# Router logits by column tiles with early weights, and the first spread of dt moved to the last expert's loads

## The chip, the cores and the metric

One core of one Trainium2 chip runs the whole network in one launch. The metric is device time in microseconds (us), the median of three executions. The engines are TensorE (PE), VectorE (DVE), ScalarE (ACT), GpSimd (POOL) and SyncE (SP, which here only issues transfers). Each works through its own list in order and waits on semaphores for the others.

## The reference, cut to what matters

Two blocks on x of shape [4, 512, 128] (2048 tokens, D = 128) come one after the other. Block 0 is attention with a gated mixture of experts; block 1 is a four-layer selective scan (state space) as `s`, and a routed mixture as `g`:

```
xn = layernorm(x)                                # end of stage 3
s  = four scan layers(xn)                        # first pieces in stage 4, the rest stage 5
h  = xn * rsqrt(mean(xn*xn) + eps)               # router input
probs  = softmax(h @ router_w.T)                 # 8 experts
p, i   = top_k(probs, 2);  rw = p / sum(p)
routed = each expert takes its first 320 tokens; silu(xg@rg) * (xg@ru) @ rd, times rw, added back
g  = silu(silu(xn@sg) * (xn@su) @ sd + routed)   # a shared expert of 1024 hidden, 8 of 512
x  = x + s * g
```

Here 2048 tokens are 16 column groups of 128 (`NT` = 16), in four chunks of 512 (`XT[:, c, :]`, x with features on partitions). `CAP` is 320.

## The kernel before

The work is a chain of stages, each a block of five instruction lists, with a barrier between blocks. The change touches the end of stage 3 (attention output, gate and layer norm of x, until about 373 us) and stage 4 (373 to 561 us). Stage 5 is the scan.

**Stage 3.** VectorE takes mean and variance of x by chunk (`mw`, `rstw`), GpSimd turns them into factors (`factors`, L1206 to L1210: a pow, then a product), ScalarE applies them (`norm_x`, L1229), TensorE transposes (`turn_x`, L1300), and ScalarE copies to `XT` (`keep_x`, L1244).

**Stage 4.** SP first loads the router's weights `w_r`, the triangle `below`, and the shared expert's `w_sg`, `w_su`, `w_sd` (L1502, L1504). TensorE waits for the first two and makes the logits as sixteen small matmuls, one for each group of 128 tokens, with x as the stationary operand and 8 columns (L1662). VectorE squares xn and sums it (L1959, L1961), GpSimd takes the root (L1608, L1609), VectorE scales the logits (L1966) and works through softmax, the two choices and the ranks. Into this chain VectorE fits `hidden` (L1957), the product of the shared expert, which TensorE needs before it can go on: a pair of gate and up matmuls (`shared`, L1670, L1671) uses two banks in turn.

Between these pairs TensorE does the first pieces of the scan (taps: `first_xi`, L1691, whose weights GpSimd builds in L1616 from a broadcast row that SP loads). GpSimd then scatters each token's row to its two experts (L1627, 32 indirect transfers, held back in groups of 11 by `s_od`).

**The experts.** Eight experts run in four rounds of two (`i` = 0, 1), each with its own buffers. TensorE does the four gate and up pairs (L1769, L1770), fetches the next expert's rows by a transpose (L1761), does the next expert's first pair, and then this expert's down product (L1794). Before an expert's first pair it waits for all three weights on one semaphore:

```
pe.wait_ge(s_w8[i], q * 48 + 48)
```

SP's list in these rounds is, for each expert, the rows, then gate and up weights, then the down weight (`turn`, L1571). Ahead of them stand the first store and spread of B and C (L1554, L1559), the rows of experts 0 and 1, and the first store of dt with its spread into `dtr_even` (L1567, L1570): four loads of 512 KB. ScalarE reads `dtr_even` as its first step of stage 5, and stage 4 ends only when the spread is in.

Of the kernel before, what the change touches and what calls it, by code (L numbers as in the profile page):

```python
# [46 lines left out]
def build_stages(nc, A, out):  # L47
    keep = ExitStack()
    with keep:
# [18 lines left out]
        tap_dram = nc.dram_tensor("taps_of_layers", [3, P, 4, 256], fp32).ap()  # L68
        keepx = ExitStack()
        X = sb(keepx, "X", [P, NT, D])  # L70
        XR = sb(keepx, "XR", [P, NT, D + 2])
# [3 lines left out]
        with keep0:  # L75
# [1086 lines left out]

            st3 = ExitStack()
            with st3:
# [15 lines left out]
                neghalf = sb(st3, "neghalf3", [P, 4])  # L1180
# [11 lines left out]
                with nc.Block() as block:  # L1192
                    @block.sync
                    def _(sp):
                        sp.wait_ge(s_es[1], 16 * (BLOCKS // 2))
                        for b in range(B):
                            sp.dma_start(part(Y1, b), yt_dram[512 * b:512 * b + 512, :].rearrange("(k p) d -> p k d", p=P)).then_inc(s_acc[b], 16)

                    @block.gpsimd
                    def _(pool):  # L1200
                        link = Chain(pool, s_pch)
                        nc.gpsimd.indirect_dma_start(yt_dram[:, :], bass.IndirectOffsetOnAxis(ap=at_t[(BLOCKS - 1) % 3][:, 0:1], axis=0), eo[(BLOCKS - 1) % 2][:, :], None,
                                                     bounds_check=T - 1, oob_is_err=False).then_inc(s_es[(BLOCKS - 1) % 2], 16)
                        link(nc.gpsimd.memset(neghalf[:, :], -0.5))

                        def factors(b, moments, r, o, turn):  # L1206
                            c = slice(4 * b, 4 * b + 4)
                            pool.wait_ge(s_st, 4 * turn + b + 1)
                            link(nc.gpsimd.tensor_tensor(r[:, c], r[:, c], neghalf[:, :], ALU.pow))
# [10 lines left out]
                        for b in range(B):  # L1220
                            factors(b, mw, rstw, ofw, 1)

# [182 lines left out]
        dtr_even = top("dtr_even", [P, 8, 512])  # L1405
# [28 lines left out]
        with st4:  # L1434
# [10 lines left out]
            w_r = sb(st4, "w_r", [P, NE])  # L1445
            w_sg = sb(st4, "w_sg", [P, 1024])
            w_su = sb(st4, "w_su", [P, 1024])
            w_sd = sb(st4, "w_sd", [P, 8, D])
# [3 lines left out]
            below = sb(st4, "below_sb", [P, P])  # L1452
# [9 lines left out]
            neghalf = sb(st4, "neghalf4", [P, NT])  # L1462
# [11 lines left out]
            sq = hid[:, 1, 0:4, :].rearrange("p a (t d) -> p (a t) d", d=D)  # L1474
# [11 lines left out]
            s_wr = sem("router_loaded")  # L1486
            s_w4, s_w8 = sem("shared_loaded"), [sem(f"expert_loaded{i}") for i in range(2)]
            s_xg = [sem(f"rows_loaded{i}") for i in range(2)]
            s_lg4, s_sq4, s_ms4, s_rn4, s_x4, s_e4, s_sel, s_rk, s_rows = map(sem, ("logits4", "squares4", "meansq4", "rnorm4", "logits_shifted", "exps4", "selected", "ranks", "rows_known"))
# [8 lines left out]
            with nc.Block() as block:  # L1498
                @block.sync
                def _(sp):  # L1500
                    for dst, src in ((w_r[:, :], A["w_router"]), (below[:, :], A["below"])):
                        sp.dma_start(dst, src).then_inc(s_wr, 16)  # L1502
                    for dst, src in ((w_sg[:, :], A["w_sg"]), (w_su[:, :], A["w_su"]), (w_sd[:, :, :], A["w_sd"])):
                        sp.dma_start(dst, src).then_inc(s_w4, 16)  # L1504

# [46 lines left out]

                    sp.wait_ge(s_dbc, 1)
# [7 lines left out]
                    sp.wait_ge(s_scat, 16 * 2 * NT)  # L1561
                    sp.wait_ge(s_clr, 12)
                    for i in range(2):
                        load_rows(i, i)

                    sp.wait_ge(s_dt, 2)
                    sp.dma_start(dt_dram[0].rearrange("(h p) t -> p h t", p=P), dt[:, :, :]).then_inc(s_dst0, 16)  # L1567
                    sp.wait_ge(s_dst0, 16)
                    for j in range(4):
                        sp.dma_start(dtr_even[32 * j:32 * j + 32, :, :], dt_dram[0].rearrange("(g c) t -> c g t", c=32)).then_inc(s_dtr0, 16)  # L1570
                    def turn(q, more):  # L1571
                        for i in range(2):

                            if more:
# [6 lines left out]
                                load_gate_up(q * 2 + (2 + i), i)  # L1581
# [1112 lines left out]
```

## Time and profile before

| | us |
|---|---|
| median of 3 runs | 1299.53 |
| lowest and highest | 1299.25, 1301.14 |
| the profiled execution | 1300.58 |
| its span, first to last instruction | 1298.7 |
| stages 1 to 3 end | about 373 |
| stage 4 | 373 to 561 |
| stage 5 and the end | 561 to 1298.7 |

The profiled execution is a fourth one, with 1.9 us around its span. Busy shares are means over stages with different limits, so a change inside stage 4 is read from the stretches of stage 4. All times below are counted from the start of the span.

### The profile page before, as it was taken

To read this page: it belongs to the slowest core of one execution; us is meant where nothing else is said; L and a number is where in the kernel's file an instruction comes from. 1 tells how busy PE (TensorE), PEld (TensorE's weight loads), DVE (VectorE), ACT (ScalarE), POOL (GpSimd) and SP (SyncE) were. 2 spreads that over 40 slices of the span, in tenths; PEclk is the share of its full clock that TensorE was granted. 3 is DMA by queue.
4 is the path that set the end of the run, shared out by engine and by line. 5 is a ranking of instruction groups with operands and counts; after the bars stand their busy time and mean duration, and the time that the engine had idled before them with its cause. 6 is when DMAs were issued, how large, how long until landed. Compare 5 with 4: busy or idle time off the path is not lost. (4 is left out here: it accounts for less than half of the span.)

```text
span 1298.7 us, 21475 instructions
## 1 busy us (share of the span) xinstructions
PE 1148.5 (88%) x6651; PEld 610.9 (47%) x6651; DVE 1085.2 (84%) x1509; ACT 1042.7 (80%) x1803; POOL 945.7 (73%) x822
## 2 busy tenths in 40 slices
PE   6467999999669999977999999999999999999885
PEld 4462245455345556743445444444444454444442
DVE  8967989999664222359999999999999999999996
ACT  4336999999642243488999999999999999999992
POOL 6733444444442541477999999999999999999995
PEclk9786999999859999989999999999999999999998
DMA  2022234343146027334325423451444254234420
GB/s 66 28 95 94 81 89 126 115 127 98 37 159 218 21 66 178 111 89 98 91 60 108 113 64 68 106 126 53 87 110 93 59 109 112 67 64 106 108 66 16
DMA packets 87972, 119.51 MB, mean 92 GB/s; under 512 B 18171, under 2 KB 48359, under 8 KB 87488
## 3 DMA queue, kind: packets, MB, share of 16 engines
q1 hardware_dynamic: 81344, 100.90, 30.7%
q0 software_dynamic: 6528, 17.40, 4.5%
q8 instruction: 48, 0.79, 0.3%
q14 instruction: 52, 0.43, 0.1%
HBM read 92.09 MB, written 27.47 MB: 92 GB/s over the span
## 5 line engine op out<-in xcount | busy, mean ns | idle before, releaser
L2212 POOL TENSOR_TENSOR hcm<-hs,Cc 128x1024 f32<-128x1024 f32 x255 | 601.0, 2381 | 27.9 <-DVE hs L2595 19.7
L2595 DVE TENSOR_TENSOR_SCAN hs<-decay,dbx 128x512 f32<-128x512 f32 x512 | 587.1, 1200 | 26.2 <-ACT decay L2488 9.5
L2329 PEld LDWEIGHTS dbx<-ident_sb,scaled 128*128 128x128 f32 x2048 | 226.8, 142 | 288.9 <-DVE hs L2595 163.5
L2329 PE MATMUL dbx<-ident_sb,scaled 128*128 128x128 f32 x2048 | 311.7, 282 | 41.9 <-DVE hs L2595 38.6
L2470 ACT ACTIVATE scaled<-duT,BT 128x256 f32<-128x256 f32 x579 | 266.5, 505 | 0.2 <-PE dbx L2329 0.2
L2488 ACT ACTIVATE decay<-dtr_odd,a_all 128x512 f32<-128x512 f32 x256 | 178.3, 723 | 3.5 <-DMA dtr_odd<-dt_turn 2.4
L2488 ACT ACTIVATE decay<-dtr_even,a_all 128x512 f32<-128x512 f32 x256 | 177.8, 717 | 3.0 <-DVE hs L2595 1.7
L2347 PE MATMUL y_bank<-hcm,fold_sb 128*32 128x512 f32 x1024 | 138.7, 614 | 1.6 <-POOL hcm L2212 1.6
L1005 ACT ACTIVATE ex<-tt 128x2048 f32<-128x2048 f32 x64 | 123.2, 1925 | 2.5 <-DVE tt L1056 1.8
L2260 PE MATMUL slots<-XT,w_tap 128*128 128x512 f32 (+1 forms) x224 | 115.4, 597 | 3.1 <-DVE scaled L2586 2.9
L2197 POOL TENSOR_SCALAR scaled<-duT,BT 128x256 f32<-128x256 f32 x204 | 96.3, 487 | 0.0
L1055 DVE TENSOR_TENSOR tt<-bank_l,gt 128x512 f32<-128x512 f32 x128 | 87.0, 680 | 6.2 <-ACT gt L998 4.5
L998 ACT ACTIVATE gt<-bank_d,dgh 128x512 f32<-128x512 f32 x128 | 82.3, 708 | 7.7 <-PE bank_d L873 7.7
L1056 DVE SCALAR_TENSOR_TENSOR tt<-bank_l,gt 128x512 f32<-128x512 f32 x128 | 86.9, 679 | 0.0
L1957 DVE TENSOR_TENSOR hid<-sil,u_bank 128x512 f32<-128x512 f32 x32 | 22.0, 687 | 59.4 <-ACT sil L1814 37.7
L927 PE MATMUL bank_pv<-ex,v_head 128*32 128x512 f32 x512 | 68.8, 611 | 2.3 <-DVE ybig L1063 1.5
L2586 DVE TENSOR_TENSOR scaled<-slots,BT 128x1024 f32<-128x1024 f32 (+1 forms) x60 | 67.8, 1130 | 0.0
L1814 ACT ACTIVATE sil<-g_bank 128x512 f32<-128x512 f32 x32 | 19.1, 597 | 47.3 <-PE u_bank L1671 47.2
L2047 DVE TENSOR_TENSOR hid<-sil,u_bank 128x320 f32<-128x320 f32 x32 | 15.6, 487 | 48.8 <-ACT sil L1900 48.8
L1635 POOL DMA_INDIRECT shares_of_tokens<-eo,to_u x18 | 17.2, 956 | 51.8 <-ACT eo L1937 48.2
L1627 POOL DMA_INDIRECT expert_rows<-XR,rows_u x32 | 31.3, 978 | 31.1 <-PE o_bank L1678 21.8
L2347 PEld LDWEIGHTS y_bank<-hcm,fold_sb 128*32 128x32 f32 x1024 | 20.3, 108 | 48.4 <-issue 40.3
(386 smaller groups left out, 1886.3 us busy)
## 6 DMA issues: line engine op xcount, KB each, us to landing
Cc<-bc_turn SPq DMA_DIRECT2D x256, 64.0 KB, 2.2
dtr_even<-dt_turn SPq DMA_DIRECT2D x32, 512.0 KB, 8.6
dtr_odd<-dt_turn SPq DMA_DIRECT2D x32, 512.0 KB, 8.9
dt_turn<-dt SPq DMA_DIRECT2D x16, 512.0 KB, 2.8
hid<-in_conv_row SPq DMA_DIRECT2D x4, 512.0 KB, 5.3
shares_of_tokens<-zeros SPq DMA_DIRECT2D x2, 1024.0 KB, 8.0
w_rg<-in_w_rg SPq DMA_DIRECT2D x8, 256.0 KB, 2.9
w_ru<-in_w_ru SPq DMA_DIRECT2D x8, 256.0 KB, 3.1
```

The source lines that it names most:

```text
L998: nc.scalar.activation(gt[:, st % RING, :], bank_d[st % 2][:, :], ACT.Tanh, scale=dgh[:, i:i + 1]).then_inc(s_G, 1)
L1005: nc.scalar.activation(ex[:, (st // 4) % 2, j:j + 2, :, :], tt[:, i:i + 2, :, :], ACT.Exp).then_inc(s_E, 2)
L1055: nc.vector.tensor_tensor(tt[:, st % RING, 0, :], bank_l[st % 2][:, 0, :], gt[:, st % RING, :], ALU.add)
L1056: nc.vector.scalar_tensor_tensor(tt[:, st % RING, 1, :], bank_l[st % 2][:, 1, :], -1.0, gt[:, st % RING, :], ALU.mult, ALU.subtract).then_ ...
L2197: nc.gpsimd.tensor_scalar(scaled[buffer_of(l, n, k)][:, kk, :, j, :], duT[:, n % 2, kk, :].rearrange("p (g c) -> p g c", c=32), BT[:, n % ...
L2212: nc.gpsimd.tensor_tensor(hcm[:, r - 1:r + 1, :], hs[:, p % HR - 1:p % HR + 1, :], Cc[:, k:k + 1, :].broadcast_to([P, 2, 512]), ALU.mult). ...
L2260: last = mm(dst[h][:, d:512], w_tap[:, 3 - d, P * h:P * h + P], XT[:, n % 4, 0:512 - d], start=(d == 0), stop=(d == 3))
L2329: last = nc.tensor.transpose(dbx[bank_of[p]][:, P * kk:P * kk + P], scaled[buffer_of(l, b, k)][:, kk, g, :, :].rearrange("p j c -> p (j c) ...
L2347: last = mm(y_bank[h][32 * q:32 * q + 32, :], fold[:, :], hcm[:, ring_of(l, b, p + q), :], start=False, stop=(k == 3), tile_position=(0, 3 ...
L2470: nc.scalar.activation(scaled[buffer_of(l, n, k)][:, kk, :, j, :], duT[:, n % 2, kk, :].rearrange("p (g c) -> p g c", c=32), ACT.Copy, sca ...
L2488: nc.scalar.activation(dec[:, p % DR, :], dtr[b % 2][:, g, :], ACT.Exp, scale=a_all[:, l, 4 * g + k:4 * g + k + 1]).then_inc(s_dec, 1)
L2595: nc.vector.tensor_tensor_scan(hs[:, p % HR, :], dec[:, p % DR, :], dbx[bank_of[p]][:, :], 0.0, ALU.mult, ALU.add).then_inc(s_sc, 1)
```

## The change

Four things are done together.

1. `dtr_even` is allocated before stage 3, and the router's, the triangle's and the shared expert's weights live in it until the shared expert is over. Their five loads are issued in stage 3.
2. The router logits come from four matmuls of 512 columns, each in its own 32 columns of the array, with the weights stationary. ScalarE copies them, four transposes turn them back, and VectorE reads them from there. The factor of the second norm, `rn_x`, is computed by GpSimd in stage 3 from the variance and factor it has; VectorE's square and sum go.
3. `hidden` stands earlier in the routing chain; scatters are held back in groups of 13 in place of 11; the rows of experts 0 and 1 are loaded ahead of the store and spread of B and C.
4. Since `dtr_even` is in use during the shared expert, the first store and spread of dt move into SP's last turn, between the gate and up weights and the down weight of expert 7. SP's loop over rounds is written out.

```diff
@@ stage 3
+            dtr_even = keepd.enter_context(nc.sbuf_tensor("dtr_even", [P, 8, 512], fp32, side="right"))
+            w_sg = dtr_even[:, 0:2, :].rearrange("p a b -> p (a b)")
...
+            w_r, below = dtr_even[:, 6, 0:32], dtr_even[:, 6, P:2 * P]
...
+                        sp.wait_ge(s_pch, 1)
+                        for dst, src in ((w_r[:, 0:NE], A["w_router"]), (below, A["below"])):
+                            sp.dma_start(dst, src).then_inc(s_wr, 16)
+                        for dst, src in ((w_sg, A["w_sg"]), (w_su, A["w_su"]), (w_sd, A["w_sd"])):
+                            sp.dma_start(dst, src).then_inc(s_w4, 16)
...
+                        link(nc.gpsimd.memset(w_r, 0.0))
...
+                        def root_of_x(b, n):
+                            c = slice(4 * b, 4 * (b + n))
+                            link(nc.gpsimd.tensor_tensor(rn_x[:, c], rstw[:, c], rstw[:, c], ALU.mult))
+                            link(nc.gpsimd.tensor_tensor(rn_x[:, c], rn_x[:, c], mw[:, c, 1], ALU.mult))
+                            link(nc.gpsimd.tensor_scalar(rn_x[:, c], rn_x[:, c], 1.1920929e-07, None, ALU.add))
+                            link(nc.gpsimd.tensor_tensor(rn_x[:, c], rn_x[:, c], neghalf[:, 0:4 * n], ALU.pow))
...
                         for b in range(B):
                             factors(b, mw, rstw, ofw, 1)
+                            if b == 1:
+                                root_of_x(0, 1)
+                        root_of_x(1, 3)
@@ stage 4, SP
-                    for dst, src in ((w_r[:, :], A["w_router"]), (below[:, :], A["below"])):
-                        sp.dma_start(dst, src).then_inc(s_wr, 16)
-                    for dst, src in ((w_sg[:, :], A["w_sg"]), (w_su[:, :], A["w_su"]), (w_sd[:, :, :], A["w_sd"])):
-                        sp.dma_start(dst, src).then_inc(s_w4, 16)
...
-                    sp.wait_ge(s_dt, 2)
-                    sp.dma_start(dt_dram[0].rearrange("(h p) t -> p h t", p=P), dt[:, :, :]).then_inc(s_dst0, 16)
-                    sp.wait_ge(s_dst0, 16)
-                    for j in range(4):
-                        sp.dma_start(dtr_even[32 * j:32 * j + 32, :, :], dt_dram[0].rearrange("(g c) t -> c g t", c=32)).then_inc(s_dtr0, 16)
+                    def spread_first_dt():
+                        sp.wait_ge(s_dt, 2)
+                        sp.dma_start(dt_dram[0].rearrange("(h p) t -> p h t", p=P), dt[:, :, :]).then_inc(s_dst0, 16)
+                        sp.wait_ge(s_dst0, 16)
+                        sp.wait_ge(s_od, at(3, 1, 1))
+                        for j in range(4):
+                            sp.dma_start(dtr_even[32 * j:32 * j + 32, :, :], dt_dram[0].rearrange("(g c) t -> c g t", c=32)).then_inc(s_dtr0, 16)
...
                                 load_gate_up(q * 2 + (2 + i), i)
+                                if q == 2 and i == 1:
+                                    spread_first_dt()
                                 sp.wait_ge(s_ed, at(q, 2, i + 1))
                                 sp.wait_ge(s_clr, 1)
                                 load_down(q * 2 + (2 + i), i)
@@ stage 4, GpSimd
-                            if (NT * i + t) % 11 == 0:
-                                pool.wait_ge(s_od, at((NT * i + t) // 11, 1, 1))
+                            if (NT * i + t) % 13 == 0:
+                                pool.wait_ge(s_od, at((NT * i + t) // 13, 1, 1))
@@ stage 4, TensorE
-                    for t in range(NT):
-                        last = mm(r_bank[:, NE * t:NE * t + NE], XT[:, t // 4, P * (t % 4):P * (t % 4) + P], w_r[:, :], start=True, stop=True)
+                    for c in range(4):
+                        last = mm(r_bank[32 * c:32 * c + 32, :], w_r, XT[:, c, :], start=True, stop=True, tile_position=(0, 32 * c), skip_group_check=True)
+                    last.then_inc(s_lg4, 1)
+                    pe.wait_ge(s_lgk, 1)
+                    for t in range(4):
+                        last = nc.tensor.transpose(x_bank[:, P * t:P * t + P], lgT[:, P * t:P * t + P], ident[:, :])
                     last.then_inc(s_lg4, 1)
@@ stage 4, ScalarE
+                    act.wait_ge(s_lg4, 1)
+                    nc.scalar.activation(lgT[:, :], r_bank[:, :], ACT.Copy).then_inc(s_lgk, 1)
@@ stage 4, VectorE
-                    TT(sq[:, :, :], XN[:, :, :], XN[:, :, :], ALU.mult).then_inc(s_sq4, 1)
...
-                    link(TT(pr[:, :, :], r_bank[:, 0:NT * NE].rearrange("p (t e) -> p t e", e=NE), wide(cols[:, 0, :]), ALU.mult))
+                    link(TT(by_chunk(pr[:, :, :]), x_bank[:, :].rearrange("p (t c e) -> p t c e", t=4, c=4)[:, :, :, 0:NE], by_chunk(wide(rn_x[:, :])), ALU.mult))
...
+                        hidden(0, i)
                         link(nc.vector.tensor_reduce(cols[:, 5, :], cand[:, :, :], AX.X, ALU.max))
                         link(TT(oh[i][:, :, :], cand[:, :, :], wide(cols[:, 5, :]), ALU.is_equal))
...
-                        hidden(0, i)
```

## Rows read from the trace of the kernel before

**Rows 1.** The page, part 1: busy us, share of the span, instructions.
```profile
PE 1148.5 (88%) x6651; PEld 610.9 (47%) x6651; DVE 1085.2 (84%) x1509; ACT 1042.7 (80%) x1803; POOL 945.7 (73%) x822
```
**Rows 2.** Windows: length, busy by engine, PEclk, DMA share, GB/s.
```profile
375.00:400.00 25.00, 24.64 (x68) 14.48 (x69) 17.27 (x41) 4.58 (x7) 11.02 (x24) 0.77 1.05 342
400.00:490.00 90.00, 88.59 (x404) 53.71 (x402) 26.42 (x49) 28.68 (x47) 37.53 (x42) 1.00 0.25 77
```
**Rows 3.** Timeline around the start of stage 4: start, length, engine, line, operation.
```profile
371.02 1.11 PE L1300 MATMUL s_bank<-ident_sb,XR 128*128 128x128 f32 x4 [1.07 <-ACT XR L1229]
...
375.31 6.99 PE L1662 MATMUL r_bank<-w_r,XT 128*128 128x8 f32 x32 [3.17 <-DMA below_sb<-in_below]
...
382.16 2.05 PE L1670 MATMUL g_bank<-XT,w_sg 128*128 128x512 f32 x2
382.42 0.29 DVE L1966 TENSOR_TENSOR pr<-r_bank,cols 128x128 f32<-128x128 f32 x1 [3.65 <-PE r_bank L1662]
...
387.24 0.69 DVE L1957 TENSOR_TENSOR hid<-sil,u_bank 128x512 f32<-128x512 f32 x1
```
**Rows 4.** Windows, the slice in which the clock rose.
```profile
386.00:388.00 2.00, 1.95 (x5) 0.45 (x4) 1.86 (x6) 0.59 (x2) 0.09 (x1) 0.90 0.94 388
```
**Rows 5.** Timeline: the last `keep_x`, and column-tile matmuls in stage 5.
```profile
372.17 0.60 ACT L1244 ACTIVATE XT<-s_bank 128x512 f32<-128x512 f32 x1 [0.72 <-PE s_bank L1300]
...
576.78 1.93 PE L2340 MATMUL y_bank<-xc,eo 128*32 128x512 f32 x8
```
**Rows 6.** Timeline: GpSimd's factors in stage 3, and the pow of 16 columns.
```profile
365.82 1.01 POOL L1209 TENSOR_TENSOR rstw<-rstw,neghalf 128x4 f32<-128x4 f32 x1 [1.56 <-DVE rstw L1334]
...
367.14 1.65 ACT L1229 ACTIVATE XR<-X,ofw,rstw 128x128 f32<-128x128 f32 x4 [0.72 <-POOL ofw L1210]
...
378.33 2.90 POOL L1609 TENSOR_TENSOR cols<-cols,neghalf 128x16 f32<-128x16 f32 x1
```
**Rows 7.** Timeline: GpSimd's first tap weights.
```profile
383.13 2.96 POOL L1616 TENSOR_TENSOR w_tap<-w_in,hid 128x256 f32<-128x256 f32 x4 [1.89 <-DMA hid<-in_conv_row]
```
**Rows 8.** Timeline of SP's list: when each transfer is issued.
```profile
488.99 1.82 SPq L1570 DMA_DIRECT2D dtr_even<-dt_turn  x4
494.67 1.62 SPq L1545 DMA_DIRECT2D xg<-expert_rows  x3
496.64 0.34 SPq L1535 DMA_DIRECT2D w_rg<-in_w_rg  x1
...
539.53 0.39 SPq L1536 DMA_DIRECT2D w_ru<-in_w_ru  x1
542.31 0.38 SPq L1540 DMA_DIRECT2D w_rd<-in_w_rd  x1
```
**Rows 9.** Transfers: us from issue to landing; the first is `dtr_even`'s, the last `w_rd`'s.
```profile
DMA to landing us min/median/max: 4.7/8.0/11.0
...
dt_turn<-dt SPq DMA_DIRECT2D x1, 512.0 KB, 2.8
...
xg<-expert_rows SPq DMA_DIRECT2D x1, 65.0 KB, 6.7
...
w_rg<-in_w_rg SPq DMA_DIRECT2D x1, 256.0 KB, 6.0
...
DMA to landing us min/median/max: 2.6/2.9/4.2
```
**Rows 10.** Timeline, TensorE: down products of experts 0 to 2; expert 7's first gate.
```profile
497.01 3.04 PE L1794 MATMUL e_bank<-w_rd,hid 128*128 128x128 f32 x24
...
506.34 2.96 PE L1794 MATMUL e_bank<-w_rd,hid 128*128 128x128 f32 x24
...
514.59 3.04 PE L1794 MATMUL e_bank<-w_rd,hid 128*128 128x128 f32 x24
...
547.25 0.78 PE L1769 MATMUL g_bank<-xgT,w_rg 128*128 128x320 f32 x2
```
**Rows 11.** Timeline, TensorE: 24 passes after a long idle time.
```profile
48.57 4.49 PE L558 MATMUL s_bank<-ident_sb,prod 128*128 128x128 f32 x24 [12.95 <-POOL prod L399]
```

More of the change, by code:

```diff
@@ L68, in build_stages @@
         tap_dram = nc.dram_tensor("taps_of_layers", [3, P, 4, 256], fp32).ap()
+        s_wr, s_w4 = (keep.enter_context(nc.semaphore(name)) for name in ("router_loaded", "shared_loaded"))
         keepx = ExitStack()
         X = sb(keepx, "X", [P, NT, D])
+        rn_x = sb(keepx, "rn_x", [P, NT])
         XR = sb(keepx, "XR", [P, NT, D + 2])
@@ L1159, in _ @@
                         settle(2, UNITS - 1)
+            keepd = ExitStack()
+            keep.push(keepd)
+            dtr_even = keepd.enter_context(nc.sbuf_tensor("dtr_even", [P, 8, 512], fp32, side="right"))
+            w_sg = dtr_even[:, 0:2, :].rearrange("p a b -> p (a b)")
+            w_su = dtr_even[:, 2:4, :].rearrange("p a b -> p (a b)")
+            w_sd = dtr_even[:, 4:6, :].rearrange("p a (f d) -> p (a f) d", d=D)
+            w_r, below = dtr_even[:, 6, 0:32], dtr_even[:, 6, P:2 * P]
             st3 = ExitStack()
@@ L1208, in factors @@
                             pool.wait_ge(s_st, 4 * turn + b + 1)
-                            link(nc.gpsimd.tensor_tensor(r[:, c], r[:, c], neghalf[:, :], ALU.pow))
+                            link(nc.gpsimd.tensor_tensor(r[:, c], r[:, c], neghalf[:, 0:4], ALU.pow))
                             nc.gpsimd.tensor_tensor(o[:, c], o[:, c], r[:, c], ALU.mult).then_inc(s_fac, 1)
@@ L1404, in build_stages @@
         dbc = top("dbc", [P, 512])
-        dtr_even = top("dtr_even", [P, 8, 512])
         scaled_0 = top("scaled_0", [P, 4, 8, 4, 32])
@@ L1485, in build_stages @@
             sem = lambda name: st4.enter_context(nc.semaphore(name))
-            s_wr = sem("router_loaded")
-            s_w4, s_w8 = sem("shared_loaded"), [sem(f"expert_loaded{i}") for i in range(2)]
+            s_w8 = [sem(f"expert_loaded{i}") for i in range(2)]
             s_xg = [sem(f"rows_loaded{i}") for i in range(2)]
-            s_lg4, s_sq4, s_ms4, s_rn4, s_x4, s_e4, s_sel, s_rk, s_rows = map(sem, ("logits4", "squares4", "meansq4", "rnorm4", "logits_shifted", "exps4", "selected", "ranks", "rows_known"))
+            s_lg4, s_lgk, s_x4, s_e4, s_sel, s_rk, s_rows = map(sem, ("logits4", "logits_copied4", "logits_shifted", "exps4", "selected", "ranks", "rows_known"))
             s_dch, s_pch, s_clr, s_zf, s_scat = map(sem, ("vector_steps4", "pool_steps4", "cleared4", "rows_cleared_x_stored", "scattered"))
@@ L1551, in _ @@
                     sp.dma_start(tap_dram[2], tap_out[:, :, :]).then_inc(s_tap, 16)
+                    sp.wait_ge(s_scat, 16 * 2 * NT)
+                    sp.wait_ge(s_clr, 12)
+                    for i in range(2):
+                        load_rows(i, i)
                     sp.wait_ge(s_dbc, 1)
@@ L1584, in turn @@
                                 load_down(q * 2 + (2 + i), i)
-                    with sp.Fori(0, 3) as q:
+                    for q in range(3):
                         turn(q, True)
@@ L1606, in _ @@
                         nc.gpsimd.memset(xg[i][:, :, :], 0.0).then_inc(s_clr, 1)
-                    pool.wait_ge(s_ms4, 1)
-                    link(nc.gpsimd.tensor_scalar(cols[:, 0, :], cols[:, 0, :], 1.0 / D, 1.1920929e-07, ALU.mult, ALU.add))
-                    nc.gpsimd.tensor_tensor(cols[:, 0, :], cols[:, 0, :], neghalf[:, :], ALU.pow).then_inc(s_rn4, 1)
                     for l in range(4):
@@ L1734, in _ @@
                     pe.wait_ge(s_sel, 1)
-                    mm(x_bank[:, 0:P], below[:, :], sel[:, :, :].rearrange("p t e -> p (t e)"), start=True, stop=False)
+                    mm(x_bank[:, 0:P], below, sel[:, :, :].rearrange("p t e -> p (t e)"), start=True, stop=False)
                     mm(x_bank[:, 0:P], ones[:, :], cum[0][:, 0:NT, :].rearrange("p t e -> p (t e)"), start=False, stop=True).then_inc(s_rk, 1)
```

21 lines of the change are left out of this document (4 added, 17 removed).

## The prediction

> **What bounds the kernel now.** I read the page first: one core, TensorE busy for 88% of the span [rows 1]. What comes after 561 us is the state-space scan, which the change leaves alone; it touches the end of stage 3 (to 373 us), stage 4 (373 to 561 us), so I asked for the busy time by stretch in stage 4. From 375 us on TensorE is busy nearly without a gap, first at a mean granted clock of 0.77 beside full DMA engines, later at 1.00 [rows 2]. Stage 4 ends in a barrier, and every engine starts stage 5 behind it. What TensorE gains or loses inside stage 4 therefore moves the end of the kernel one for one, and I price each edit by when TensorE starts its next matmul.
>
> Then the timeline of the boundary. The last turn of x runs at 371.02 us, the next matmul at 375.31: TensorE waits for `w_r` and `below`, loaded only when stage 4 begins. Thirty-two 8-column matmul passes take 6.99 us, and the first matmul of the shared expert stands at 382.16; VectorE takes the logits at 382.42 [rows 3]. From there TensorE works through without a stall worth counting until the experts. The clock is at its lower level (1.2 GHz) until about 386.4 us: the slice from 386 to 388 us has a mean of 0.90 [rows 4]. So it rose some 4.2 us after 382.16, when dense matmuls had replaced the narrow ones.
>
> **Part A, the router at the front.** After the change the weights are in SBUF before stage 4, so TensorE starts with the first other engines, at about 373.3 us.
> - Four column-tile matmuls of 512 columns, eight passes, stand side by side. The nearest row is the same form (128x32 weights, 512 columns, eight passes) near a low clock: 1.93 us. The copy of 128x512 on ScalarE is the 0.60 us of `keep_x` [rows 5]. Four transposes at the lower clock are 1.11 us [rows 3]. With two hand-overs of about 0.05 us (the ScalarE copy at 372.17 begins as the modelled matmul end of 371.02 + 1.11 passes) that is 1.93 + 0.60 + 1.11 + 0.1 = 3.7 us.
> - What it costs ahead of that: GpSimd computes `rn_x` in stage 3. One pow of 4 columns is 1.01 us (365.82 to 366.83); the product behind it is over when ScalarE goes on at 367.14, so a small product with its gaps is about 0.28, and the new group `root_of_x(0, 1)` is 3 x 0.28 + 1.09 = 1.9 us. It starts at 364.3 and ends at 366.2, where the factors of the third group started at 365.82 and ScalarE stood waiting for them. So the stage-3 chain slips 0.4 us (0 if the gaps are shorter, 0.6 if longer). The last group is 12 columns; a pow of 16 columns took 2.90 us, so about 2.3, and 369.3 + 0.9 + 2.3 = 372.5 us, behind the last `keep_x` (372.8) and so hidden [rows 6].
> - Sum: 373.3 + 0.4 + 3.7 = 377.4 us for the first shared matmul, against 382.16. **Gain 4.7 us.** Bounds: 5.2 with nothing lost in stage 3; 4.0 if the clock rises later after a front that is now broken up by a hand-over (1.4 us more at half clock would cost 0.7).
> - Does it stay? VectorE drops a product and a sum over 2048 elements that were hidden anyway, and its first `hidden`, which stood 4.8 us behind the start of the routing chain [rows 3], now stands three steps earlier in it. Even at the old distance it runs from 377.6 + 4.8 = 382.4 to 383.1, and TensorE needs it only after two pairs of gate and up, 5.8 us in the kernel before (382.16 until that `hidden` was over at 387.93): 383.2. The tap weights could become the next wait: GpSimd began them at 383.13 when the broadcast row landed, 2.96 us for four [rows 7]. That load is now issued about 1.9 us earlier with 1.5 MB less in front. Landing at 378.5 to 381.2 gives taps at 381.5 to 384.2, against a need at 377.4 + 5.8 + 1.7 = 384.9. Covered, narrowly at one end.
> - The five loads moved into stage 3 stand behind the four loads of Y1 in an idle queue; nobody there waits behind them. Scatters regrouped from 11 to 13 end sooner and the expert rows were not late before: worth nothing. Storing and spreading B and C behind the rows is hidden too, since Cc is read in stage 5 alone.
>
> **Part B, the early spread goes.** Before, SP issued the four 512 KB loads of `dtr_even` from 488.99 us; the rows of the third expert were issued at 494.67 [rows 8]. The last spread load landed 11.0 us after its issue at about 490.4, so at 501.4, and the rows landed 6.7 us after theirs, at 501.4 as well [rows 9]. The first expert's down product starts at 497.01, the second's 9.33 us later, the third's 8.25 us after that [rows 10]. The period without the collision is 8.25. **Gain 1.1 us** (0.9 to 1.3).
>
> **Part C, where the spread goes to.** This edit decides. `spread_first_dt` is now issued inside the last turn of SP's list, between `load_gate_up` and `load_down` of the last expert. Ahead of `load_down(7, 1)` stand a 512 KB store, a wait for its landing, and the four loads. TensorE needs all three weights of expert 7 before its first gate product: `s_w8[1]` must reach 192, which counts `w_rd`. That product ran at 547.25 us [rows 10], and `w_rd` had been issued at 542.31 [rows 8] and landed in 2.9 [rows 9], about 2 us ahead. On the time scale of before:
> - store issued at 540.0 us, behind `w_ru` (issued 539.53). It alone took 2.8 us [rows 9], giving 542.8; behind two 256 KB loads still moving until about 542.1, I take 544.0.
> - the first spread load goes at 544.0, and the last lands 501.4 - 488.99 = 12.4 us later, at 556.4. `w_rd`, issued at 546.1 (the four issues take 1.82 us [rows 8]), is behind it: `w_rg` of before, issued next after the rows, landed at 496.64 + 6.0 = 502.6, 1.2 us after them [rows 8, 9]. I take 1.0: 557.4.
> - TensorE stands still from 547.25 to 557.4. **Loss 10.1 us** (8.9 if the store lands at 542.8; 10.6 if the homeward scatters of GpSimd slow it). Nothing hides it: TensorE issues in order, the down product of expert 6 is behind the same wait, and ScalarE, VectorE and the barrier behind that.
>
> The Trainium skill (DMA: Bandwidth & Descriptors, "Queues, rings and completion order") says that descriptors are consumed in ring order on each engine, and SP owns one row of rings. By that rule `w_rd` cannot pass the spread; the trace agrees, with the rows and the last spread load both landing at 501.4 us. Without the rule the forecast would be the first rival below.
>
> - **The clock after that stall.** After 12.95 us of idling, TensorE's 24 passes at 48.57 us took 4.49 us [rows 11], where 24 passes take 3.0 in the experts [rows 10]: 1.5 us lost. The rise at 386.4 came after 4.2 us at half clock, 2.1 us lost. **Loss 1.8 us** (1.0 to 3.0).
>
> The Trainium skill (TensorE: Matmul & The Clock Gate, "What's actually happening") says that the slow clock is the default and activity releases it. By that rule an idle stretch is paid again when work comes back; the trace agrees with the 1.5 us above. A sum that left it out would be 1.8 us lower.
>
> **Sum.** -4.7 - 1.1 + 10.1 + 1.8 = +6.1 us. The profiled execution took 1300.58 us in all, 1.05 above the median of the three runs; applied to the median, 1299.53 + 6.1 = 1305.6 us. With all bounds on one side: +3.4 (1302.9) to +8.7 (1308.2); that is the likeliest case's own range.
>
> **Rivals.**
> - *`w_rd` overtakes the spread* (ends on the other side). If transfers of one queue share the engines instead of queueing, `w_rd` is issued at 546.1 and lands 4.2 us later, the longest of its six [rows 9]: 550.3, a stall of 3.1 with hardly a clock to lose: -4.7 - 1.1 + 3.1 = -2.7, 1296.8 us. It decides for faster once `w_rd` lands before about 553 us on the old scale. Against it: the rows and the spread's end coincide. For it: the two loads differ in shape. With it goes the case that I misplace the need and TensorE waits later. Chance 0.12.
> - *The front gives nothing.* If the column tiles ran one after another, eight passes at half clock (the 2.05 us pair [rows 3] times four, 8.2 us) take 6.3 us more than assumed, and A turns into a loss of 1.6: +12.4, 1311.9 us. Milder: the taps late by 1 to 2 us or the clock late, A of 2 to 3 us, about 1308. For it: the taps have 0.7 us of cover at one end. Against: the column-tile row. Chance 0.10.
> - *The stall is shorter than I sum*, by a faster late spread, since then the experts' loads are nearly over: 7 us and 1 of clock, +2.2, 1301.7 us. Against it: the early one moved alone for most of its time as well. Chance 0.10.
> - My forecast: 0.68.
>
> **Numbers.** A measurement of this kernel tells about 0.2%, 2.6 us, from no change: 1296.9 to 1302.1. The overtaking case lies half below that; the short stall is inside. Faster 0.09, same 0.15, slower 0.76. The range takes in the forecast's bounds, most of the short stall and the milder front loss: 1301.0 to 1309.0, leaving out the overtaking case and the serial tiles.
>
> **What would show it.** Right: the first shared matmul 4 to 5 us earlier; no wait for rows at the third expert; SP's list with store, spread, then `w_rd` last; a TensorE wait of 9 to 10 us on `w_rd` ahead of the eighth expert's gate product; a clock of 0.5 behind it. Wrong: `w_rd` landing ahead of the last spread load; a wait for the broadcast row at the taps; transposes of the logits that start after 377 us.

## The result, and the profile after

| | before | after |
|---|---|---|
| median of 10 runs each, us | 1300.38 | 1304.21 |
| lowest and highest, us | 1299.25, 1302.78 | 1303.93, 1305.44 |
| profiled execution, its span, us | 1300.58, 1298.7 | 1305.44, 1303.6 |

The ratio of the times is 1.0031, with a 95% interval of 1.0022 to 1.0040: slower by 0.3%, on the forecast's side of the 0.2% bound. The sum had said 1305.6 us, and the range 1301.0 to 1309.0.

The front in the profile after, from the timeline (start, length, engine, line, operation, idle time and its releaser):

```profile
371.64 0.60 ACT L1270 ACTIVATE XT<-s_bank 128x512 f32<-128x512 f32 x1 [0.73 <-PE s_bank L1326]
...
373.28 1.94 PE L1676 MATMUL r_bank<-XT,dtr_even 128*32 128x512 f32 x8 [1.68 <-PEq L1202]
...
375.92 1.11 PE L1680 MATMUL x_bank<-ident_sb,logits_by_expert 128*128 128x128 f32 x4 [0.71 <-ACT logits_by_expert L1826]
...
376.83 1.92 PE L1688 MATMUL g_bank<-XT,dtr_even 128*128 128x512 f32 x2
...
377.42 0.73 POOL L1630 TENSOR_TENSOR w_tap<-w_in,hid 128x256 f32<-128x256 f32 x1 [1.00 <-DMA hid<-in_conv_row]
```

The four column tiles take 1.94 us, and the first shared matmul stands at 376.83, where it stood at 382.16 [rows 3]: 5.3 us earlier. Of these, 0.8 were there before the change begins (the same instruction of stage 3, ahead of GpSimd's new steps, stood at 360.13 before and at 359.36 after), so the front itself gave 4.6. Below, profiles are laid against each other at ScalarE's last copy of stage 3, the first line here (371.64; 372.17 before, [rows 5]). The tap weights begin at 377.4, 5.7 us ahead of [rows 7]. Neither they nor the first `hidden` (381.18) hold TensorE up.

The clock, from the windows of the profile after (length, busy by engine, PEclk, DMA share, GB/s):

```profile
380.00:382.00 2.00, 2.00 (x4) 0.87 (x3) 1.51 (x5) 0.60 (x1) 0.29 (x1) 0.63 1.01 427
382.00:384.00 2.00, 2.00 (x6) 0.89 (x5) 1.79 (x7) 0.60 (x1) 0.00 (x0) 1.00 0.38 61
...
544.00:546.00 2.00, 0.00 (x0) 0.00 (x0) 0.00 (x0) 0.00 (x0) 0.00 (x0) 0.83 1.10 206
546.00:548.00 2.00, 0.00 (x0) 0.00 (x0) 0.00 (x0) 0.00 (x0) 0.00 (x0) 0.50 1.04 239
...
554.00:556.00 2.00, 2.00 (x12) 1.88 (x12) 0.00 (x0) 0.11 (x1) 0.00 (x0) 0.61 0.00 0
556.00:558.00 2.00, 2.00 (x12) 1.59 (x13) 0.00 (x0) 0.87 (x3) 0.00 (x0) 1.00 0.00 0
```

The clock rose in the slice from 380 us, some 4.6 us after the first shared matmul (4.2 before). It fell to its lower level in the slice from 544 us, when TensorE had idled since 540.6, and was back at 2.4 GHz by 556.

The experts, TensorE's timeline after:

```profile
491.51 3.04 PE L1812 MATMUL e_bank<-w_rd,hid 128*128 128x128 f32 x24
...
508.00 3.04 PE L1812 MATMUL e_bank<-w_rd,hid 128*128 128x128 f32 x24
...
539.86 0.70 PE L1788 MATMUL u_bank<-xgT,w_ru 128*128 128x320 f32 x2
550.37 1.41 PE L1787 MATMUL g_bank<-xgT,w_rg 128*128 128x320 f32 x2 [9.81 <-DMA w_rd<-in_w_rd]
...
552.63 4.37 PE L1812 MATMUL e_bank<-w_rd,hid 128*128 128x128 f32 x24
556.93 0.81 PE L1787 MATMUL g_bank<-xgT,w_rg 128*128 128x320 f32 x2
...
561.72 3.07 PE L1812 MATMUL e_bank<-w_rd,hid 128*128 128x128 f32 x24 [1.05 <-DVE hid L2064]
566.93 1.50 PE L2346 MATMUL dbx<-ident_sb,scaled 128*128 128x128 f32 x12 [2.15 <-PEq L1516]
```

Each stage of the sum can be read off against [rows 10]. The first down product is 5.50 us earlier, the third 6.59: the early collision is gone, 1.1 us. Then comes the wait of 9.81 us, named as forecast, and expert 7's first gate product is 3.12 us later than before instead of 6.6 earlier, so the stall took 9.7. From it to the pair behind the down product are 6.56 us; before they were 4.04 (547.25 to 551.29), so the low clock took 2.5. Stage 5 begins 5.6 us later than at 561.30; in this execution it was itself 0.7 us shorter, so the span grew by 4.9.

SP's list after, and how long two of its transfers took:

```profile
532.90 0.43 SPq L1581 DMA_DIRECT2D dt_turn<-dt  x1
537.18 1.83 SPq L1585 DMA_DIRECT2D dtr_even<-dt_turn  x4
539.11 0.53 SPq L1553 DMA_DIRECT2D w_rd<-in_w_rd  x1
```

```profile
dt_turn<-dt SPq DMA_DIRECT2D x1, 512.0 KB, 4.3
...
w_rd<-in_w_rd SPq DMA_DIRECT2D x1, 256.0 KB, 11.2
```

`w_rd`, 256 KB, is issued at 539.11 and lands 11.2 us later, at 550.3, where it took 2.9 [rows 9]. The last of the spread's four loads lands at about 549.7 (issued at 538.6, 11.1 us to its landing), ahead of it.

### The profile page after: what moved, and what is told of

The parts are those of the page before. It is cut to its first block and busy times, and to the rows that moved or that the text cites. A ratio compares the mean times of both kernels' runs of the same rounds, so it can differ in the third digit from the quotient of the medians.

```text
span 1303.6 us, 21361 instructions
## 1 busy us (share of the span) xinstructions
PE 1148.3 (88%) x6631; PEld 609.1 (47%) x6631; DVE 1079.6 (83%) x1507; ACT 1042.5 (80%) x1804; POOL 945.8 (73%) x828
```

## The experiments

My theory: the front and the lost collision give some 6 us, and the stall of TensorE on `w_rd` with its clock takes some 12. Rivals: the end of stage 4 is set by something else, so that taking the stall away gives back less; and the front gives less or more than its parts.

**x1. The spread behind the down weight.**

```diff
                                 load_gate_up(q * 2 + (2 + i), i)
-                                if q == 2 and i == 1:
-                                    spread_first_dt()
...
                                 load_down(q * 2 + (2 + i), i)
+                                if q == 2 and i == 1:
+                                    spread_first_dt()
```

> The changed kernel with the store and spread of dt moved by one place, behind the load of expert 7's down weight. Queue theory (the loss is only w_rd's place behind the store and the spread): the wait of 9.8 us and the 2.5 us of low clock behind it go; GpSimd's scatters home still share the engines with the spread and may now end the stage, costing 0 to 1.5 us. 1304.2 - 12.2 + 0.8 = about 1293 us (1291.5 to 1295). Load theory (2 MB late in stage 4 hurt wherever they stand, by full transfer engines): most of the loss stays, 1300 us or more. Time theory (the spread would now be late for stage 5): a ScalarE wait ahead of the first decay, 1297 or more.

Measured: 1296.47 us, ratio 0.9971 (0.9961 to 0.9981). The wait on `w_rd` is gone, yet only two thirds of the 12 us came back: above the range of the Queue theory, and well below the 1300 us of the Load theory. The timeline of x1:

```profile
544.19 3.66 POOL L1661 TENSOR_SCALAR scaled<-duT,BT 128x256 f32<-128x256 f32 x8 [4.85 <-DMA shares_of_tokens<-eo,to_u]
...
547.92 3.07 PE L1812 MATMUL e_bank<-w_rd,hid 128*128 128x128 f32 x24 [1.05 <-DVE hid L2064]
...
550.65 0.93 POOL L1666 DMA_INDIRECT shares_of_tokens<-eo,to_u  x1 [0.30 <-issue]
...
556.27 3.41 PE L2346 MATMUL dbx<-ident_sb,scaled 128*128 128x128 f32 x16 [5.28 <-PEq L1516]
```

TensorE is done at 550.99 and waits 5.28 us at the barrier, where it waited 2.16 before. GpSimd is the late one. It waits for the scatters of expert 5's rows to land, 4.85 us (before: 1.62), where the spread is in flight beside them (x11 gives the 1.62 us back with no spread there); then it computes `scaled_0` for 3.66 us, and only then issues the scatters of expert 6. From the end of its last one (551.58) to stage 5 are 4.69 us. That distance is 4.68 us before the change (556.62 to 561.30) and in the profile after (562.25 to 566.93), too. The prediction left this list out.

**x2. The spread ahead of the rounds, as before the change.** 
```diff
-                                if q == 2 and i == 1:
-                                    spread_first_dt()
...
+                    spread_first_dt()
                     for q in range(3):
                         turn(q, True)
```

> The changed kernel with the store and spread of dt ahead of the expert rounds, as in the kernel before. Queue theory: no wait for w_rd, and the 1.1 us wait of the third expert's rows is back: 1304.2 - 12.2 + 1.1 = about 1293 us (1292 to 1296). The front's gain then stands alone against the kernel before: 5 to 7 us faster. If the front had gained nothing: 1300.

Measured: 1295.83 us, ratio 0.9960 (0.9946 to 0.9975). TensorE's timeline of x2:

```profile
490.38 3.04 PE L1811 MATMUL e_bank<-w_rd,hid 128*128 128x128 f32 x24
...
496.68 0.64 PE L1778 MATMUL x_bank<-ident_sb,xg 128*128 128x128 f32 x3 [1.99 <-DMA xg<-expert_rows]
...
500.82 1.39 PE L1811 MATMUL e_bank<-w_rd,hid 128*128 128x128 f32 x11
```

The first two down products are 10.44 us apart in place of 8.24: the early collision costs 2.2 us here, since TensorE arrives sooner; the expectation had 1.1 for it, and its range held. There is no stall at the end.

**x3. The late spread alone**, moved in the kernel before, whose front stays as it was.

```diff
@@ kernel before
+                    def spread_first_dt():
...
                                 load_gate_up(q * 2 + (2 + i), i)
+                                if q == 2 and i == 1:
+                                    spread_first_dt()
```

> The kernel before with one edit only: the store and spread of dt in the last turn, ahead of expert 7's down weight. Queue theory: +9.7 (wait) + 2.5 (clock) - 1.1 (early collision gone) = +11.1, about 1311.5 us (1309.5 to 1313). If the loss needed the other edits (the weights' new place, the reordered queue): less than +5.

Measured: 1311.60 us, ratio 1.0082 (1.0064 to 1.0100). TensorE's timeline of x3:

```profile
554.70 1.41 PE L1772 MATMUL g_bank<-xgT,w_rg 128*128 128x320 f32 x2 [10.15 <-DMA w_rd<-in_w_rd]
```

TensorE waits 10.15 us for `w_rd`. The harm needs none of the other edits: the spread's place alone costs 10.7 us net by the ratio (8.3 to 13.0).

**x4. The down weight on a semaphore of its own.** The gate product needs `w_rg` and `w_ru` alone; only the down product waits for `w_rd`. The transfers stand as after.

```diff
-                            pe.wait_ge(s_w8[i], q * 48 + 48)
+                            pe.wait_ge(s_w8[i], q * 32 + 32)
...
+                            pe.wait_ge(s_wd[i], q * 16 + 16)
                             pe.wait_ge(s_hd8, n(4, 4))
```

> The changed kernel with the down weight on a semaphore of its own, which TensorE waits for ahead of the down product instead of ahead of the first gate product. The transfers keep their order. Queue theory: w_rd lands at about 550.3 us, needed at about 549.4 now, so a wait of some 1 us, no low clock, GpSimd perhaps the last: 1293 to 1296 us. Load theory: full engines still delay what comes, 1300 or more.

Measured: 1298.32 us, ratio 0.9985 (0.9971 to 0.9998); the time lies over 2 us above the expected range. The timeline of x4:

```profile
547.83 3.68 POOL L1661 TENSOR_SCALAR scaled<-duT,BT 128x256 f32<-128x256 f32 x8 [7.42 <-DMA shares_of_tokens<-eo,to_u]
549.90 3.07 PE L1813 MATMUL e_bank<-w_rd,hid 128*128 128x128 f32 x24 [1.96 <-DMA w_rd<-in_w_rd]
...
554.30 0.94 POOL L1666 DMA_INDIRECT shares_of_tokens<-eo,to_u  x1 [0.30 <-issue]
...
559.93 2.37 PE L2347 MATMUL dbx<-ident_sb,scaled 128*128 128x128 f32 x10 [6.96 <-PEq L1516]
```

TensorE waits only 1.96 us for the weight and is done at 552.97. Then it waits 6.96 us for GpSimd, whose last scatter ends at 555.24, 4.69 us ahead of stage 5. So the stall on `w_rd` had hidden a second one, on the scatters home, and this bears out x1's reading.

**x5. x1, with `scaled_0` computed between the issue of expert 5's scatters and the wait for them.**

```diff
-                    def send_home(q, i):
+                    def send_home(q, i, meanwhile=lambda: None):
...
+                        meanwhile()
                         pool.wait_ge(s_eh, q * 96 + 48 * (i + 1))
...
+                    send_home(2, 1, first_scaled)
```

> The first experiment (spread behind the down weight) with one more edit: GpSimd computes its eight parts of scaled_0 while expert 5's scatters home are in flight, not behind their landing. In the first experiment GpSimd's last scatter stood 7.8 us behind the start of expert 6's down product, against 4.6 where no spread was in flight, and stage 5 started 4.65 us after GpSimd's last scatter in every trace. Theory (GpSimd's list, held up by scatters that share the engines with the spread, ended stage 4): 3.1 us less, about 1293.4 us (1292.5 to 1295). Rival (the spread's own landing or a second wait ends the stage): within 1 us of the first experiment's 1296.5.

Measured: 1293.71 us, ratio 0.9943 (0.9929 to 0.9956). The timeline of x5:

```profile
540.63 3.66 POOL L1660 TENSOR_SCALAR scaled<-duT,BT 128x256 f32<-128x256 f32 x8
...
547.75 1.06 POOL L1671 DMA_INDIRECT shares_of_tokens<-eo,to_u  x1 [3.46 <-DMA shares_of_tokens<-eo,to_u]
...
550.38 0.94 POOL L1671 DMA_INDIRECT shares_of_tokens<-eo,to_u  x1 [0.30 <-issue]
...
556.00 3.13 PE L2351 MATMUL dbx<-ident_sb,scaled 128*128 128x128 f32 x16 [3.76 <-PEq L1516]
```

The wait at the barrier shrank from 5.28 to 3.76 us by a change of GpSimd's order alone; its last scatter again ends 4.68 us ahead of stage 5. GpSimd's list sets the end of stage 4: in all thirteen profiles its last scatter ends 4.67 to 4.69 us ahead of stage 5, also in x1, x4 and x5, where TensorE's own wait is 5.28, 6.96 and 3.76 us instead of the 2.15 of the others. What fills these 4.68 us is not shown.

The profile has 1.5 us of gain over x1 where the expectation had 3.1: expert 5's scatters landed 7.16 us after the end of their issue here and 4.85 in x1, and why is not shown. The ratios differ by 3.6 us, with some 2 us of noise either way, which leaves room for both. So the direction is shown and the size is not.

**x6. TensorE kept busy through the wait**, by eleven matmuls of no use ahead of it. They write a bank that is written anew before it is read.

```diff
                             pe.wait_ge(s_tc, at(q, 2, i + 1))
+                            if i == 1 and isinstance(q, int) and q == 3:
+                                for _ in range(11):
+                                    mm(x_bank[:, :], ident[:, :], XT[:, 0, :], start=True, stop=True)
                             pe.wait_ge(s_w8[i], q * 48 + 48)
```

> The changed kernel with 11 extra matmuls of 512 columns (22 passes, about 9.5 us at full clock) into a free bank ahead of TensorE's wait for expert 7's weights; their result is read by nobody. Clock theory: the wait's end stays (w_rd's landing), the clock stays at full, and the 24 passes of the down product take 3.0 us, not 4.4: 2.5 us less, about 1301.7 us. Rival (what follows the wait is slow for another reason, such as full transfer engines): no change, 1304.2.

Measured: 1303.77 us, ratio 1.0022 (1.0013 to 1.0032). TensorE's timeline of x6:

```profile
539.27 9.60 PE L1787 MATMUL x_bank<-XT,ident_sb 128*128 128x512 f32 x22
549.34 0.81 PE L1790 MATMUL g_bank<-xgT,w_rg 128*128 128x320 f32 x2 [0.47 <-DMA w_rd<-in_w_rd]
...
550.52 2.97 PE L1815 MATMUL e_bank<-w_rd,hid 128*128 128x128 f32 x24
...
563.41 1.50 PE L2349 MATMUL dbx<-ident_sb,scaled 128*128 128x128 f32 x12 [2.15 <-PEq L1516]
```

The weight comes no sooner (58.96 us behind the first down product, 58.86 after), the granted clock is 1.00 in every slice from 538 to 552 us, and from the gate product to stage 5 are 14.07 us, where the profile after has 16.56 and the one before 14.05: in the profile, the 2.5 us are the clock's. The times say less. Their median is nearer the rival's 1304.2 than the 1301.7 expected, and the profiled execution is the fastest of the ten. By the ratios the gain is 1.2 us with some 1.7 of noise either way: it holds both nothing and 2.5.

**x7. The sixteen small matmuls of before**, all else as after; ScalarE's copy goes too, and VectorE reads `r_bank`.

```diff
-                    for c in range(4):
-                        last = mm(r_bank[32 * c:32 * c + 32, :], w_r, XT[:, c, :], start=True, stop=True, tile_position=(0, 32 * c), skip_group_check=True)
...
-                        last = nc.tensor.transpose(x_bank[:, P * t:P * t + P], lgT[:, P * t:P * t + P], ident[:, :])
+                    for t in range(NT):
+                        last = mm(r_bank[:, NE * t:NE * t + NE], XT[:, t // 4, P * (t % 4):P * (t % 4) + P], w_r[:, 0:NE], start=True, stop=True)
```

> The changed kernel with the logits as before, sixteen matmuls of 8 columns, from the weights loaded early, and no copy and no transposes. By the rows: 7.0 us in place of 3.6 from the first logits matmul to the first shared one, so +3.4: about 1307.5 us (1306 to 1309). Rival (the column tiles gain nothing, the early weights everything): 1304.

Measured: 1309.46 us, ratio 1.0066 (1.0050 to 1.0081). TensorE's timeline of x7:

```profile
372.53 6.97 PE L1676 MATMUL r_bank<-dtr_even,XT 128*128 128x8 f32 x32 [1.68 <-PEq L1202]
379.35 2.05 PE L1684 MATMUL g_bank<-XT,dtr_even 128*128 128x512 f32 x2
```

6.82 us from the first logit to the shared expert in place of 3.55: the new form gives 3.3 us here, and 4.0 until the first down product (122.18 us from the first logit, 118.23 after). By the ratios it gives 4.5, so the time lies a little above the expected range.

**x8. The five weight loads at the head of stage 4**, all else as after.

```diff
@@ stage 3, SP
-                        for dst, src in ((w_r[:, 0:NE], A["w_router"]), (below, A["below"])):
-                            sp.dma_start(dst, src).then_inc(s_wr, 16)
...
@@ stage 4, SP, its first instructions
+                    for dst, src in ((w_r[:, 0:NE], A["w_router"]), (below, A["below"])):
+                        sp.dma_start(dst, src).then_inc(s_wr, 16)
+                    for dst, src in ((w_sg, A["w_sg"]), (w_su, A["w_su"]), (w_sd, A["w_sd"])):
+                        sp.dma_start(dst, src).then_inc(s_w4, 16)
```

> The changed kernel with the five weight loads back at the head of stage 4; column tiles stay. By the rows: TensorE waits until 375.3 of before, 2.0 us later than now, and the broadcast row for the taps lands some 5 us later but still in time: +2.0, about 1306.2 us. If the taps become the wait: 1307 to 1309. Rival (the weights' load was hidden by something else): 1304.

Measured: 1307.48 us, ratio 1.0052 (1.0037 to 1.0067). TensorE's timeline of x8:

```profile
370.53 0.60 ACT L1265 ACTIVATE XT<-s_bank 128x512 f32<-128x512 f32 x1 [0.73 <-PE s_bank L1321]
...
373.70 1.93 PE L1676 MATMUL r_bank<-XT,dtr_even 128*32 128x512 f32 x8 [3.21 <-DMA dtr_even<-in_below]
...
378.94 2.07 PE L1688 MATMUL g_bank<-XT,dtr_even 128*128 128x512 f32 x2 [1.47 <-DMA dtr_even<-in_w_sd]
```

Two waits instead of one: 3.21 us for `below`, and 1.47 for `w_sd`, since logits that are done sooner meet shared weights that are not there. The expectation left out the second one.

From the last copy of stage 3 to the first shared matmul are 8.41 us here and 5.19 after, so the loads' place gives 3.2 us (2.7 by the ratios). The bare times, 378.94 and 376.83, differ by 2.1 only because stage 3 ended 1.1 us sooner in this execution. The same distance is 9.99 us before and 8.47 in x7. So neither edit has one price: the early loads give 1.5 us with the old logits and 3.2 with the new ones, and the new logits give 1.6 with late loads and 3.3 with early ones. Together they give 4.8.

**x9. Only the store of dt moved ahead of the rounds**; the spread stays where after has it.

```diff
                     def spread_first_dt():
-                        sp.wait_ge(s_dt, 2)
-                        sp.dma_start(dt_dram[0].rearrange("(h p) t -> p h t", p=P), dt[:, :, :]).then_inc(s_dst0, 16)
...
+                    sp.wait_ge(s_dt, 2)
+                    sp.dma_start(dt_dram[0].rearrange("(h p) t -> p h t", p=P), dt[:, :, :]).then_inc(s_dst0, 16)
                     for q in range(3):
```

> The changed kernel with only the store of dt moved ahead of the expert rounds (it finds an idle queue); the four spread loads keep their place ahead of w_rd. Queue theory: SP no longer stops for the store's landing, so the spread is issued at 532.9 us in place of 537.2, its last load and w_rd land 4.3 us earlier, and the wait is 5.5 us in place of 9.8: 4.3 us less, 1299.9 us (1299 to 1301); a shorter idle time may save some clock too. Load theory (the bytes late in stage 4 are the cost): 1303 or more, since only 0.5 MB moved away.

Measured: 1302.06 us, ratio 1.0015 (1.0004 to 1.0026). The timeline of x9:

```profile
532.31 1.94 SPq L1583 DMA_DIRECT2D dtr_even<-dt_turn  x4
535.06 0.40 SPq L1553 DMA_DIRECT2D w_rd<-in_w_rd  x1
...
546.94 1.41 PE L1787 MATMUL g_bank<-xgT,w_rg 128*128 128x320 f32 x2 [7.04 <-DMA w_rd<-in_w_rd]
```

The wait is 7.04 us in place of 9.81: not the whole of the store's 4.3 comes back, and the time lies 1 us above the expected range, yet below the Load theory's 1303 as well. Counted from the first down product the spread goes out 4.2 us sooner, but from its issue to the end of the wait are 14.6 us, where after has 13.2. Here the spread stands directly behind `w_rg` and `w_ru`, issued at 531.21 and 531.78, which may slow its start; no run tests that. `w_rd`, issued at 535.06, lands last again, 11.8 us later.

**x10. `hidden` back in its old place, and the scatters in groups of 11.**

```diff
-                            if (NT * i + t) % 13 == 0:
-                                pool.wait_ge(s_od, at((NT * i + t) // 13, 1, 1))
+                            if (NT * i + t) % 11 == 0:
+                                pool.wait_ge(s_od, at((NT * i + t) // 11, 1, 1))
...
-                        hidden(0, i)
                         link(nc.vector.tensor_reduce(cols[:, 5, :], cand[:, :, :], AX.X, ALU.max))
...
+                        hidden(0, i)
```

> The changed kernel with hidden back at the end of each choice and the scatters back in groups of 11. Both were priced at nothing: TensorE's third pair needs the first hidden 0.3 to 1.0 us after it is over, and the last scatter ends some 10 us ahead of the first expert's rows. 1304.2 us, within 0.7. Rival: with the front 5 us earlier the later hidden holds TensorE up, up to 1 us, and the scatters hold up the rows, 1 to 3 us more.

Measured: 1306.20 us, ratio 1.0044 (1.0030 to 1.0059). TensorE's timeline of x10, and below it the same pair in x11:

```profile
382.51 1.12 PE L1688 MATMUL g_bank<-XT,dtr_even 128*128 128x512 f32 x2 [0.84 <-DVE hid L1977]
```

```profile
381.71 1.12 PE L1688 MATMUL g_bank<-XT,dtr_even 128*128 128x512 f32 x2
```

The third shared pair waits 0.84 us for `hidden`. The profile after is no measure for that, since its clock rose 2.2 us later: its third pair starts at 382.58, no sooner than here. In x11 the clock rose as early as here and `hidden` stands in its new place, and from the first logit to the first down product are 117.44 us, here 118.21. So the place of `hidden` is worth 0.8 us where the clock rises early, and by these rows nothing where it rises as late as in the profile after: even in its old place the first `hidden` is over at 382.46, ahead of 382.58. The last scatter of rows went out at 471.98 us in place of 466.84, and no row was late for it.

The time lies 1.3 us above the expected range, on the side of the rival. By the ratios the two edits give 1.7 us, with some 2 of noise either way, so no more than the 0.8 can be assigned.

**x11. The spread taken apart**: dt stored ahead of the rounds, and one of the four loads behind the down weight of each of the first four turns.

```diff
                                 load_down(q * 2 + (2 + i), i)
+                                if q < 2:
+                                    spread_part_of_dt(2 * q + i)
```

> The kernel after with dt stored ahead of the rounds and its spread taken apart: one 512 KB load behind the down weight of each of the first four turns, none in the last. My account: what costs is the pile of four loads in front of a weight or a row that is needed soon. One load has to pass in the 3.1 us between the down weight and the next rows, and the rows have some 7 us until TensorE turns them. Then no wait on xg or w_rd appears on TensorE, the down products stand 8.24 us apart throughout, GpSimd's wait for the scatters of expert 5 is 1.6 us as before, and stage 5 begins 63.2 us after the first down product (65.4 in x2, less its collision of 2.2): span about 1290 to 1292, time about 1293.5 us, ratio 0.9945. Rival: any 2 MB of spread costs its share wherever it stands, since each later transfer of the turn is moved back: then the 2.2 us of x2 come back in small waits and the time is that of x2, about 1296 us (0.996).

Measured: 1293.70 us, ratio 0.9950 (0.9937 to 0.9964). The timeline of x11:

```profile
490.73 3.04 PE L1812 MATMUL e_bank<-w_rd,hid 128*128 128x128 f32 x24
...
493.80 0.38 SPq L1553 DMA_DIRECT2D w_rd<-in_w_rd  x1
494.27 0.45 SPq L1583 DMA_DIRECT2D dtr_even<-dt_turn  x1
496.69 1.33 SPq L1558 DMA_DIRECT2D xg<-expert_rows  x3
...
541.75 3.66 POOL L1661 TENSOR_SCALAR scaled<-duT,BT 128x256 f32<-128x256 f32 x8 [1.62 <-DMA shares_of_tokens<-eo,to_u]
...
553.92 1.50 PE L2346 MATMUL dbx<-ident_sb,scaled 128*128 128x128 f32 x12 [2.15 <-PEq L1516]
```

Stage 5 begins 63.19 us after the first down product (65.39 in x2, 75.42 after), GpSimd's wait is 1.62 us as before the change, and TensorE waits for no transfer. The same 2 MB cost nothing that is seen when they pass one part at a time. This version and x5 are faster than the kernel before by 0.50% and 0.57%, alike within their intervals.

## Why the prediction came right

- **The bound** (TensorE inside stage 4) held up to the last expert. What ends the stage it left out: GpSimd's last scatter, 4.67 to 4.69 us ahead of stage 5 in all thirteen profiles. In the change itself this costs nothing beyond the forecast, since those scatters wait for expert 6's down product and slip with it. It cost me the expectations of x1 and x4.
- **Part A**, 4.7 us: the profile has 4.6 at the first shared matmul. Its terms miss a little and cancel. The first logit comes 1.5 us sooner behind stage 3 where the sum had 2.0, the logits take 3.3 us less where it had 3.15, and stage 3 slips 0.2 where it had 0.4. "Eight passes side by side" held (1.94 us against 1.93 in [rows 5]). The Trainium skill (TensorEngine Tiling (Array Packing), "Key Properties") says that tiles operate independently and can work in parallel; the trace agrees, since one full matmul of two passes takes as long (1.92 us). What the sum did not have: the clock mostly rose sooner than assumed (below). With an early rise, as in x11, A is 5.5 us at the first down product instead of the 4.7 of the profile after, and the move of `hidden`, priced at nothing, is worth 0.8 of them.
- **Part B**, 1.1 us: measured 1.1. It was a lower figure than the collision is worth behind the new front (2.2, x2).
- **A and B together** are x11: 6.5 us by its ratio (4.7 to 8.2), 6.6 by its profile, where the sum had 5.8.
- **Part C, the stall**, 10.1 us: the profile has 9.7. The store took 4.3 us (assumed: 4.0), `w_rd` was issued 6.2 us behind it (6.1) and landed last, as the prediction had it: 11.2 us for 256 KB.
- **Part C, the clock**, 1.8 us: the profile has 2.5, above the middle of its bounds of 1.0 to 3.0.
- **C over many runs** is the ratio of after less that of x11, 10.5 us, where the sum had 11.9 and the two profiles show 12.2 (75.42 less 63.19 us from the first down product to stage 5). The two intervals leave some 2 us either way, so the profiles' 12.2 is inside. By the ratios, then, the +4.0 differ from the forecast +6.1 by 1.4 us in C and 0.7 in A and B; the noise is as large as that, and which term was off is not shown.
- **One execution is not the median.** The ten times after fall into six from 1303.93 to 1304.25 us and four from 1305.12 to 1305.44, and the profiled one is of the upper four. What parts the groups is not shown. One candidate is the clock at the front. In the nine profiles with this front it rose 4.6 us (after), 4.2 (x4), 3.9 (x2) and 2.0 to 2.5 us (the other six) behind the first shared matmul, from the mean clock of the slice in which it rose. But the late rise costs less than its time at half clock, because with an early one TensorE waits shortly for `hidden` (0.17 us in x1 and x9, 0.27 in x6): from the first logit to the first down product are 118.23 us after, 117.36 to 117.59 in the five profiles with an early rise and the new place of `hidden`. That is 0.6 to 0.9 us, and the groups stand 1.2 apart.
- **One profile is not a time.** From the start of stage 5 to the end of the span, with the same instructions, the thirteen profiles have 736.5 to 739.1 us. A gain of 1 or 2 us in stage 4 can therefore be read from the stretch in which it arises, not from the span of one execution.

The rivals: overtaking is out (`w_rd` landed last after, in x3 and in x9), so are serial tiles (1.94 us for all four), and the stall was not much shorter (9.81 us).

## What to carry to other kernels

A transfer list in order is a list of due times: before a bulk load is moved, ask what stands behind it in the queue and when that is needed. Here a store of 512 KB, the wait for its landing and 2 MB ahead of one 256 KB weight cost 10.5 us; with the store out of the way it was some 2 us less (x9). The same 2 MB in four parts, each in the gap between one expert's last weight and the next expert's rows, cost nothing that was seen. When a stall is taken away, look for the list that was late beside it (here GpSimd's scatters, slowed by the same transfers), and judge a gain of 0.3% by many runs, not by the span of one.

## What the runs showed of the hardware

- GpSimd's scatters beside SP's spread: from the end of issue to the wait's end 1.62 to 1.63 us without it (before, x2, x11), 4.85 (x1) to 7.68 (x7) with it. But the scatters landed ahead of the spread's end (548.36 us, the last spread load at about 549.7). The Trainium skill (DMA: Bandwidth & Descriptors, "SWDGE vs HWDGE vs iDMA") says that the two kinds of queue feed different internal queues of an engine, which takes turns between them. The trace agrees: slowed, not held back to the end.
- The spread moved at 205 to 239 GB/s with the engines' share at 1.04 to 1.10 (windows 540 to 548 us after). The loads at the front reach 427 at a share of 1.01. By these windows, in which GpSimd's scatters move too, a byte of the spread costs an estimated twice the engine time of a byte of a weight.
- The clock rises and falls at no fixed distance from what TensorE does. It rose 2.0 us (x5) to 4.6 us (after) behind the first shared matmul, with the same instructions up to there, and fell after 2.5 us of idling in x10, 4.8 after and 5.3 in x7.
